# Last layer of a graph network: the rows of the destination nodes by one-hot products on TensorE instead of gathers

## What is computed

```
msg_s = (s_n @ Ws_src)[src] + (s_n @ Ws_dst)[dst]
msg_v = einsum('ncx,cd->ndx', v_n, Wv_src)[src] + einsum('ncx,cd->ndx', v_n, Wv_dst)[dst]
w1 = rbf @ W_rbf
m1_s, m1_v = _cg_tp(msg_s, msg_v, y0, y1, w1[...])     # products with the edge's direction
a = leaky(m1_s @ W_alpha) ...; val_s = m1_s @ Ws_val; val_v = m1_v by Wv_val, gated by a sigmoid
m2_s, m2_v = _cg_tp(val_s, val_v, y0, y1, w2...)
hs = m2_s @ Ws_vlin; hv = m2_v by Wv_vlin               # 64 scalars, 32 vectors an edge
```

## Time and profile before

| | us |
|---|---|
| median of three runs | 7715.1 |
| lowest and highest | 7669.87, 7729.05 |
| span of the profiled execution | 7980.6 |
| first pass of the last layer in it | 2792 (4588 to 7380) |

### The profile page before, as it was taken

The page is one execution under the profiler, slowest core; times in us unless marked ns, Lnnn a source line. Parts: engine busy times, 40 slices in busy tenths (PEclk is TensorE's granted clock), DMA queues, the critical chain, the costliest instruction groups (busy, mean ns, idle before and its releaser), DMA issues. The chain is left out here.

```text
span 7980.6 us, 110610 instructions
## 1 busy us (share of the span) xinstructions
PE 7037.4 (88%) x32406; PEld 4813.5 (60%) x32406; DVE 6580.0 (82%) x18417; ACT 3693.0 (46%) x9602; POOL 5364.8 (67%) x4078
## 2 busy tenths in 40 slices
PE   6999999997999999899999788888888888888488
PEld 3444444444555555555555477777787777777366
DVE  7999999996788888688888677777787777777785
ACT  2444444443333333433333355555555555555385
POOL 1777777773577777377777188888888888887000
PEclk7999999996899999799999778888888888888698
DMA  7999999998222222122222133322222222222263
GB/s 211 167 168 170 167 169 165 166 162 189 52 65 66 66 65 61 37 68 69 69 69 69 32 68 76 73 68 71 73 76 69 74 70 72 72 72 71 68 192 107
DMA packets 459687, 776.87 MB, mean 97 GB/s; under 512 B 96721, under 2 KB 310966, under 8 KB 458838
## 3 DMA queue, kind: packets, MB, share of 16 engines
q0 software_dynamic: 274944, 469.50, 32.1%
q1 hardware_dynamic: 180038, 299.69, 12.3%
q10 hardware_dynamic: 4112, 0.62, 0.1%
HBM read 464.60 MB, written 304.85 MB: 96 GB/s over the span
## 5 line engine op out<-in xcount | busy, mean ns | idle before, releaser
L1446 DVE TENSOR_TENSOR work<-work 128x256 f32<-128x256 f32 (+5 forms) x5726 | 2483.9, 472 | 70.3 <-DMA work<-src_sum 27.6
L624 POOL DMA_INDIRECT fore<-node_table,src_i x1664 | 1709.7, 1027 | 655.9 <-issue 504.4
L662 POOL DMA_INDIRECT src_sum<-work,put_i x832 | 1325.2, 1593 | 557.1 <-ACT work L836 384.6
L624 POOL DMA_INDIRECT fore<-src_table,src_i x784 | 1218.3, 1554 | 406.8 <-issue 238.6
L624 POOL DMA_INDIRECT fore<-dst_table,dst_i x784 | 1090.0, 1390 | 238.9 <-issue 238.9
L1233 PE MATMUL bank<-work 128*128 128x384 f32 (+1 forms) x3328 | 1198.8, 503 | 10.4 <-DVE work L1446 10.4
L1330 PE MATMUL bank<-ident,work 128*128 128x128 f32 x4704 | 733.5, 297 | 444.4 <-DVE work L1446 444.4
L1233 PEld LDWEIGHTS bank<-work 128*128 128x128 f32 x3328 | 603.2, 191 | 688.2 <-issue 313.6
L1446 DVE TENSOR_TENSOR work<-work,bank 128x384 f32 (+6 forms) x2080 | 908.0, 437 | 78.4 <-issue 70.7
L1330 PEld LDWEIGHTS bank<-ident,work 128*128 128x128 f32 x4704 | 572.3, 151 | 566.7 <-DVE work L1446 506.0
L848 ACT ACTIVATE work<-bank 64x512 f32<-64x512 f32 x416 | 245.8, 591 | 1436.6 <-PE bank L1200 1436.6
(11 more groups left out here) (246 smaller groups left out, 13200.5 us busy)
## 6 DMA issues: line engine op xcount, KB each, us to landing
edge_h<-work SPq DMA_DIRECT2D x196, 320.0 KB, 2.3
work<-edge_h SPq DMA_DIRECT2D x196, 320.0 KB, 3.4
work<-keys SPq DMA_DIRECT2D x196, 256.0 KB, 5.8
fore<-node_table,src_i POOLq DMA_INDIRECT x1664, 2.7
work<-in_edge_attr SPq DMA_DIRECT2D x196, 128.0 KB, 5.9
src_sum<-work SPq DMA_DIRECT2D x4, 6240.0 KB, 37.5
work<-src_sum SPq DMA_DIRECT2D x100, 240.0 KB, 4.3
src_sum<-work,put_i POOLq DMA_INDIRECT x832, 5.9
```

The source lines that it names most:

```text
L624: return pool.indirect_dma_start(dst, None, table, bass.IndirectOffsetOnAxis(ap=idx, axis=0), bounds_check=bound, oob_is_err=True)
L662: pool.indirect_dma_start(src_sum[t], bass.IndirectOffsetOnAxis(ap=put_i[:, e:e + 1], axis=0), E.run[:, g % 2, t * 480:(t + 1) * 480], Non ...
L1446: return V_.tensor_tensor(o, p, q, op)
```

## The change

The destination rows are no longer gathered. VectorE compares the dst keys of a tile, broadcast to all partitions by a DMA (`dst_keys`), with the row numbers of the tile's window (`turned`, four operations a group, three groups ahead). TensorE multiplies this one-hot matrix with the window of `skip` (`dst_rows`), into banks 4 and 5, which hold one group. `m1` adds the product from PSUM to the rows gathered by src. To free the two banks, the transposes of m2 go to banks 1 and 2 as well, and each transpose waits until ScalarE has copied what the other left there. The window is now that of a tile's first key. For a lane whose dst lies past the border of the window (24 borders), the product gives zero; its src row is replaced by a row that already has the dst row added. These 24 x 128 rows are gathered from both tables at the start of the pass, the second time adding, and written behind `src_table`; their indices are made in `border_tiles`, one step a group on VectorE in the second layer's stage. The maps val_x, val_yz, lin_x and lin_yz are multiplied by their 64 filled columns only.

```diff
+                for k in range(MORE):
+                    gather(T.border[:, k, :], src_table[0:ROWS], border_src_i[:, k:k + 1], last_row).then_inc(s.border_src_in, 16)
+
+                pool.wait_ge(s.border_src_in, 16 * MORE)
+                for k in range(MORE):
+                    pool.indirect_dma_start(T.border[:, k, :], None, dst_table, bass.IndirectOffsetOnAxis(ap=border_dst_i[:, k:k + 1], axis=0),
+                                            compute_op=ALU.add, bounds_check=last_row, oob_is_err=True).then_inc(s.border_rows, 16)
+
+                pool.wait_ge(s.border_kept, 16)
...
-                        gather(T.gs[:, b, t, :], src_table, src_i[:, e:e + 1], last_row).then_inc(
+                        gather(T.gs[:, b, t, :], src_table, put_i[:, e:e + 1], last_src_row).then_inc(
                             got[3][b], 16)
-                        gather(T.gd[:, b, t, :], dst_table, dst_i[:, e:e + 1], last_row).then_inc(
-                            got[3][b], 16)
...
+                def dst_keys(g):
+                    b = g % 2
+                    if g >= 2:
+
+                        sp.wait_ge(s.dst_turned, g - 1)
+                    sp.dma_start(T.keys[:, b].rearrange("p t n -> p (t n)"),
...
-                unrolled(GROUPS, [(0, rbf), (5, keep_h)])
+                for g in range(2):
+                    dst_keys(g)
+
+                sp.wait_ge(s.border_rows, 16 * MORE)
+                sp.dma_start(src_table[ROWS:ROWS + MORE * P].rearrange("(k p) c -> p k c", p=P), T.border).then_inc(s.border_kept, 16)
+                unrolled(GROUPS, [(0, rbf), (-2, lambda g: dst_keys(g) if g >= 2 else None), (5, keep_h)])
...
                         pe.wait_ge(s.m1_done, h // 2 + 1)
+                    if h >= 4:
+
+                        pe.wait_ge(s.m2_in_sbuf, h - 3)
...
+                def dst_rows(h):
+                    g, at = h // 2, h % 2 * 2
+                    if h % 8 == 0:
+                        n = min(16, TILES - 2 * h)
+                        pe.load(held[0:n], tile_window_i[0:1, 2 * h:2 * h + n])
+                    if at == 0:
+
+                        pe.wait_ge(s.dst_turned, g + 1)
+                        if g:
+
+                            pe.wait_ge(s.rows_added, g)
+                    for t in range(2):
+                        window = pe.snap(held[(2 * h + t) % 16], min_val=0, max_val=WINDOWS - 1)
+                        last = nc.tensor.matmul(gd[:, at + t, 0:DIM], T.turned[:, g % 2, at + t, :],
+                                                skip[:, bass.ds(window, 1), 0:DIM].rearrange("p o c -> p (o c)"),
+                                                start=True, stop=True)
+                    last.then_inc(s.dst_rows_mm, 1)
...
-                        nc.tensor.matmul(o[:, 164:292], t1[:, t, 128:256], wt["val_x"][:], start=True, stop=False)
-                        last = nc.tensor.matmul(o[:, 164:292], t1[:, t, 256:384], wt["val_yz"][:], start=False, stop=True)
+                        nc.tensor.matmul(o[:, 164:228], t1[:, t, 128:256], wt["val_x"][:, 0:64], start=True, stop=True)
+                        last = nc.tensor.matmul(o[:, 228:292], t1[:, t, 256:384], wt["val_yz"][:, 64:128], start=True, stop=True)
...
-                    turn3(T.f2, h, 4, s.m2_turned)
+
+                    pe.wait_ge(s.m1_in_sbuf, min(h + 4, TILES // 2))
...
+                    turn3(T.f2, h, 1, s.m2_turned)
...
-                unrolled(TILES // 2, [(-3, turn_m1), (1, linear), (-3, values), (0, turn_m2), (-6, edge_w3)])
+                gd = dst_rows_mm()
+                unrolled(TILES // 2, [(-3, turn_m1), (1, linear), (-3, values), (-5, dst_rows), (0, turn_m2), (-6, edge_w3)])
...
+                    if l == 1 and g >= 8:
+                        next(border, None)
...
-                    dve.wait_ge(got[3][depth], (g // DEPTH + 1) * (16 * 2 * GROUP))
-                    tt(m, T.gs[:, depth], T.gd[:, depth], ALU.add).then_inc(s.rows_added, 1)
+                    dve.wait_ge(got[3][depth], (g // DEPTH + 1) * (16 * GROUP))
+
+                    dve.wait_ge(s.dst_rows_mm, 2 * g + 2)
+                    tt(m, T.gs[:, depth], gd[:, :, 0:DIM], ALU.add).then_inc(s.rows_added, 1)
...
-                unrolled(GROUPS, [(-1, m1), (0, m2), (2, edge_out)])
+                gd = dst_rows_mm()
+
+                def turned(g):
...
+                    for t in range(GROUP):
+                        e = g * GROUP + t
+                        last = V_.tensor_scalar(T.turned[:, b, t, :], T.keys[:, b, t, :], src_f[:, e:e + 1], None, ALU.is_equal)
+                    last.then_inc(s.dst_turned, 1)
+                unrolled(GROUPS, [(-1, m1), (0, m2), (-3, turned), (2, edge_out)])
```

More of the change, by code:

```diff
@@ L319, in l3_views @@
             v.rb = g(2, 512)
-            rows = fore[:, 0:DEPTH * 8 * DIM].rearrange("p (b k t c) -> p b k t c", b=DEPTH, k=2, c=DIM)
-            v.gs, v.gd = rows[:, :, 0], rows[:, :, 1]
+            v.gs = fore[:, 0:2560].rearrange("p (b t c) -> p b t c", b=DEPTH, c=DIM)
+            v.keys = fore[:, 2560:3584].bitcast(I32).rearrange("p (b t n) -> p b t n", b=2, n=P)
+            v.turned = fore[:, 3584:4608].rearrange("p (b t n) -> p b t n", b=2, n=P)
             v.m = g(GROUP, DIM)
@@ L324, in l3_views @@
             v.cv = g(2, GROUP, 196)
+            at_f = g.used()
             v.f, v.f2 = g(2, GROUP, 352), g(2, GROUP, 352)
+            v.border = work[:, at_f:at_f + MORE * DIM].rearrange("p (k c) -> p k c", c=DIM)
             v.t1, v.t2 = g(2, 2, 384), g(2, 2, 384)
@@ L337, in build, with border_views, get @@
         T = l3_views()
+        def border_views():
+            flat = aux[:].rearrange("p t c -> p (t c)")
+            at = [0]
+            def get(n):
+                at[0] += n
+                assert at[0] <= ALL_TILES * 5
+                return flat[:, at[0] - n:at[0]]
+            v = type("Border", (), {})
+            v.firstI, v.window, v.one, v.lower, v.src = get(TILES).bitcast(I32), get(TILES), get(TILES), get(TILES), get(TILES)
+            v.before, v.none, v.shift, v.dst, v.inside, v.mask, v.rest, v.row = (get(MORE) for _ in range(8))
+            v.tile_i = get(MORE).bitcast(I32)
+            return v
+        B = border_views()
         def pass2_views():
@@ L482, in table_out @@
                 tables = ((node_table[l], fore[:, 0:SLOTS * DIM].rearrange("p (j c) -> p j c", j=SLOTS)),) if l < 3 else \
-                    ((src_table, fore[:, 0:SLOTS * DIM].rearrange("p (j c) -> p j c", j=SLOTS)), (dst_table, skip[:, :, 0:DIM]))
+                    ((src_table[0:ROWS], fore[:, 0:SLOTS * DIM].rearrange("p (j c) -> p j c", j=SLOTS)), (dst_table, skip[:, :, 0:DIM]))
                 for j0, j1 in HALVES:
@@ L1368, in linear @@
                         nc.tensor.matmul(o[:, 0:64], t2[0:96, t, 0:128], wt["lin_s"][:], start=True, stop=True)
-                        nc.tensor.matmul(o[:, 64:192], t2[:, t, 128:256], wt["lin_x"][:], start=True, stop=False)
-                        last = nc.tensor.matmul(o[:, 64:192], t2[:, t, 256:384], wt["lin_yz"][:], start=False, stop=True)
+                        nc.tensor.matmul(o[:, 64:128], t2[:, t, 128:256], wt["lin_x"][:, 0:64], start=True, stop=True)
+                        last = nc.tensor.matmul(o[:, 128:192], t2[:, t, 256:384], wt["lin_yz"][:, 64:128], start=True, stop=True)
                     last.then_inc(s.linear_mm, 1)
-                unrolled(TILES // 2, [(-3, turn_m1), (1, linear), (-3, values), (0, turn_m2), (-6, edge_w3)])
+                gd = dst_rows_mm()
+                unrolled(TILES // 2, [(-3, turn_m1), (1, linear), (-3, values), (-5, dst_rows), (0, turn_m2), (-6, edge_w3)])
                 barrier(pe, "pe")
@@ L1499, in _ @@
             V_.tensor_scalar(U.lane, spare[:], 1.0, -float(ROWS), ALU.mult, ALU.add).then_inc(dve_own, c.step())
+            V_.tensor_scalar(lane[:], spare[:], 1.0, -float(ROWS), ALU.mult, ALU.add).then_inc(dve_own, c.step())
             big = Nv.big.rearrange("p (j c) -> p j c", c=DIM)
@@ L1865, in edges_by_window @@
                         V_.memset(W.msg[:, b].rearrange("p (t c) -> p t c", c=385)[:, :, 384:385], 1.0).then_inc(dve_own, c.step())
+                border = border_tiles()
                 unrolled(ALL_GROUPS, [(0, stage)])
+                assert l > 1 or next(border, True)
                 add(2 * ALL_GROUPS - 3)
```

95 lines of the change are left out of this document (91 added, 4 removed).

## The result

The changed kernel takes 9826.8 us (four runs, 9821.3 to 9845.2) against 7708.9 us: 1.275 times the kernel before, interval 1.270 to 1.279. The direction was forecast; the size, 8580, was not, and lies far outside the range. The profiled execution of the changed kernel is 9823.1 us long, as the timed ones.

The account below looks back on a forecast made before the run. GpSimd's gathers were taken to bound the kernel's last-layer first pass. 7980.6 - 2792 + 3420 (196 groups of 17.45) + 92 + 11 = 8712 us; the middle between that and 8447 gave 8580, range 8200 to 8760.

Parts of the forecast that it names:

- The bound, and what its relief is worth: Last layer's first pass: GpSimd's gathers set 14.2 us a group; relieving them is worth at most 3.3 us a group.
- rival 2: Last layer's first pass: loop not closed, VectorE alone sets the period, 12.2 us; median about 7550 us; chance 0.08.
- The loop: TensorE and VectorE take turns through dst_rows and m1: period 17.45 us a group against 14.2, TensorE idle 3.4 us.
- The cold stretch: After each group's wait of 3.4 us, TensorE runs at 1.2 GHz for the first 5.7 us.
- The narrow maps: TensorE's values with 64-wide maps: 0.62 us a tile, 1.24 instead of 1.45 us a half.
- The shared banks: Transposes of m1 and m2 sharing PSUM banks: nothing added, 0.16 us to spare, bound above 0.4 us a half.
- Border rows and second layer: Border rows before the pass's first gather cost 92 us; border_tiles on VectorE in the second layer costs 11 us.
- The 265 us: Runs' median lies 265 us under the profiled span; the forecast took the middle of 8447 and 8712 us, 8580.
- Rival 3: Maps narrowed to 64 columns take half: about 1.2 us a group, 240 us less, so 8340 us; chance 0.04.

Follow-up runs that it names:

- lag -6: The changed kernel with dst_rows one iteration (half a group) earlier in TensorE's list, -6 in place of -5: 7927 us, 0.977 of the kernel before.
- lag -7: The changed kernel with the four maps 128 columns wide and dst_rows at -7 in place of -5 in TensorE's list: 9046 us, 1.191 of the kernel before.
- wait filled: The changed kernel plus 14 unread matmuls of 128 columns on TensorE before each wait for m1_done: 8599 us, 1.061 of the kernel before.

## Why the prediction was wrong

- *The bound, and what its relief is worth.* Right in kind. GpSimd paced the pass; with the loop open (lag -6) VectorE and TensorE pace it at 11.8 us, near the forecast of rival 2 (12.2) for that case. But the 14.2 us a group were those of one long execution: 2512 us are 12.8 a group, so there was less to gain than 3.3 us.
- *The loop.* Right in mechanism, place and sizes: `m1` 5.0, waits of 2.1 to 3.9 us in each group, and 15.2 us at full clock where the steps give 15.0. Shown by opening it (0.977) and by filling the wait (15.2 us). One sentence on it was wrong: "There is one buffer, so no half can be earlier." At lag -6 both halves stand one iteration earlier with the same one buffer, the wait for `rows_added` is met by then, and the kernel is 0.977 of the one before; only at -7 is it too early.
- *The cold stretch: the step that failed.* "So I take 1.2 GHz for the first 5.7 us of every group." That length was read from a group with wide maps and carried over to a program whose maps the same change had narrowed. There the clock comes back only after 10 us (41 groups) or 20 us and more (152 groups), and the period is 23.1 us on average where 17.45 were forecast: 5.65 us times 196, 1107 us. At 1.2 GHz throughout, the steps are 10.9 us for the first iteration (6660.35 to 6671.28), 7.8 to the end of `dst_rows`, 5.1 for `m1`: 23.8, and 24.0 is measured. That the narrowed maps did it in this kernel is shown: with wide maps and such a wait in each group 16.8 to 17.3 us a group (0.84 clock), and narrow maps alone cost 1.157 in the kernel before. That the widths are not the whole of it is shown too: 1.013 with all four narrow and two unread products, at most 1.010 with one pair narrow, and 10 us of cold stretch with wide maps at lag -7. What of the stream of instructions decides the length stays open.
- *The narrow maps.* Forecast 0.62 us a tile for the values; 0.73, as before. The 0.17 us from lin_s to the next is not what each 64-wide map takes: in the rows after, the starts stand 0.17 to 0.23 us apart. It would have been a small error, were it not for the clock.
- *The shared banks.* Forecast at nothing; 1.005 alone (some 40 us), and no wait for ScalarE among the long ones after.
- *Border rows and second layer.* 88 and 11 us, for 92 and 11.
- *The 265 us.* The forecast split them, half in the pass. The first trace has 5197 us outside the pass (7980.6 - 2784). The changed kernel's trace, an execution as long as its timed ones, has 5314 outside (9823.1 less 4688 to 9197), and 5215 without the 88 and 11 us in front of its pass: the same to 0.4 per cent. So the profiled execution before was long in its gather-bound pass, by nearly all of the 265 us (7708.9 - 5197 = 2512). The right base was 8712, not 8580; this is the other 132 us of the 1247 missed.
- *The chances.* None of the rivals was this one. Rival 3 asked whether narrow maps are cheaper than thought and found no harm in them; that a change in a matmul's shape changes how long the clock stays down was not thought of. Nor was a rival given for a longer cold stretch of any cause, although the whole sum hung on one such row.

The difference to the kernel before, taken apart on one kind of chip: 10145 (changed) to 8958 (wide maps), 1187 us for the clock that narrow maps hold down; 8958 to 8599 (wait filled), 359 for the cold stretches that the waits still leave; 8599 to 7927 (lag -6), 672 for the turns; and 7927 is 176 under the kernel before beside it, 8103, which is what the gathers were worth after some 90 us of border rows. The wait is filled and the lag moved with narrow maps, so the border between the first two steps is rough; and 10145 was measured in a later set on that chip, where the kernel before took 8082.

## What to carry to other kernels

Before a product is moved between two engines, walk the semaphore cycle that it closes: from one engine's signal, through the other's list in program order, back to the same signal one step on; its length is a floor for the period, and half a step in the list can be worth a quarter of the time. Where an engine waits in each step, the length of a cold stretch measured with one set of matmul shapes and one order may not be carried to another, and narrowing a matmul that is not paced by its columns saves nothing (0.73 us a tile in both forms here). If a stretch stays at half clock though TensorE is always busy, test it with a few unread matmuls before optimising anything else.

## What was not expected of the hardware

- A stream can run at half clock for 3800 us though TensorE is busy for 3783.70 of them: the kernel before with four narrow maps, which starts its pass at half clock. The lag -6 kernel with narrow maps starts its pass at half clock too, and is at 1.00 after 78 us. The two differ in `dst_rows`, two more products a half, among other things. Whether the first stream would stay at full clock if it began its pass at full clock was not run.
- With all four maps narrow and two more products a half the clock is 0.88, without the two 0.50; with one pair narrow 0.88 (values) or 0.87 (linear); with none 0.91.
- A chip can be a seventh slower in the middle layers: their gathers take 2684 us (2083 to 4767) on one, 2353 (2067 to 4420) on another. The gathers of the last layer do not follow: mean 1.29 and 1.21 us on the first of these, 1.28 and 1.22 on the chip of 7607 us. The 1.55 and 1.39 of the earlier trace rows belong to the one long execution.
